# Second attention of a four-stage block: score passes of two heads as 64-row tiles, keys stored without zero halves

## The reference

```python
q = (x @ wq).reshape(B, T, H, D)              # H = 16 heads, D = 8, T = 256
lat = x @ w_down                              # 64 wide
k = (lat @ wk_up).reshape(B, T, H, D)
v = (lat @ wv_up).reshape(B, T, H, D)
q, k = _apply_rope(q, cos, sin), _apply_rope(k, cos, sin)
scores = jnp.einsum('bqhd,bkhd->bhqk', q, k) * scale
allowed = pages[None, :] <= pages[:, None]    # pages of 32 tokens
scores = jnp.where(allowed[None, None], scores, jnp.finfo(scores.dtype).min)
attn = jax.nn.softmax(scores, axis=-1)
out = jnp.einsum('bhqk,bkhd->bqhd', attn, v).reshape(B, T, E)
return out @ wo
```

## Time and profile before

| | us |
|---|---|
| median of 3 runs (lowest, highest) | 507.35 (506.74, 508.24) |
| the profiled execution | 500.75 |
| its span, first to last instruction | 498.9 |
| PE / VectorE (DVE) / ScalarE (ACT) / GpSimd (POOL) busy | 427.2 / 317.1 / 240.6 / 217.4 |
| mean granted clock of TensorE | 0.92 of full speed |

### The profile page before, as it was taken

One profiled execution on the slowest core, in us unless ns is written; L12 is line 12 of the kernel. 1 busy time (PEld: TensorE's weight loads), 2 busy tenths in 40 slices (PEclk: granted clock), 3 DMA queues, 4 the chain that ended last, 5 costly groups with the idle time before them and its releaser, 6 DMA issues.

```text
span 498.9 us, 15441 instructions
## 1 busy us (share of the span) xinstructions
PE 427.2 (86%) x5122; PEld 342.5 (69%) x5123; DVE 317.1 (64%) x1181; ACT 240.6 (48%) x575; POOL 217.4 (44%) x313
## 2 busy tenths in 40 slices
PE   8989899998668999976769989999899887899990
PEld 8767687886557899853546666666667666689980
DVE  4756588887554555279466567577777756555543
ACT  2676656765304555111325756657566440155540
POOL 5433345554633444324742625526531444334440
PEclk9989999997758999987678999999999997699996
DMA  8899900000001122120000000000000000112216
GB/s 263 273 210 347 292 13 11 6 11 12 23 16 44 55 63 63 55 57 1 2 1 1 1 3 2 0 0 0 1 1 3 18 28 22 32 51 64 63 47 179
DMA packets 43443, 29.12 MB, mean 58 GB/s; under 512 B 7200, under 2 KB 39456, under 8 KB 43264
## 3 DMA queue, kind: packets, MB, share of 16 engines
q1 hardware_dynamic: 37200, 21.35, 15.2%
q0 software_dynamic: 2496, 5.13, 2.8%
q10 hardware_dynamic: 3696, 1.97, 1.4%
HBM read 13.29 MB, written 15.16 MB: 57 GB/s over the span
## 4 chain that ended last, share of the span: by engine, by line
PE 60%; DVE 14%; issue 8%; ACT 7%; DMA 7%; DVEq 2%; POOL 2%; SPq 0%; ACTq 0%; POOLq 0%
PE S L1433 6%; PE S L1341 6%; PE bank L1300 6%; PE bank L1443 5%; PE bank L1317 3%; PE S L1520 3%; ACT E L1008 3%; PE S L1521 3%; PE bank L1473 3%; DMA slots<-yo,token 3%; PE bank L1533 2%; PE bank L1496 2%; PE bank L1327 2%; PE S L1273 2%; PE bank L1246 2%
## 5 line engine op out<-in xcount | busy, mean ns | idle before, releaser
L913 ACT ACTIVATE E<-S,nmax 128x256 f32<-128x256 f32 x128 | 59.0, 477 | 40.7 <-DVE nmax L541 38.0
L1148 POOL DMA_INDIRECT slots<-yo,token x46 | 44.1, 958 | 68.1 <-DVE yo L697 66.8
L1008 ACT ACTIVATE E<-S 128x1536 f32<-128x1536 f32 x32 | 46.4, 1451 | 25.3 <-PE S L1524 25.3
L1105 POOL TENSOR_TENSOR vs<-Va,rden 128x512 f32<-128x512 f32 x32 | 33.3, 1040 | 54.6 <-DVE rden L576 53.1
L1433 PE MATMUL S<-xgT,W1s 128*128 128x128 f32 x368 | 51.3, 282 | 1.4 <-DVE xgT L683 1.3
L757 DVE TENSOR_REDUCE nm<-bank 128x2 f32<-128x512 f32 x64 | 41.1, 683 | 15.9 <-PE bank L1496 15.9
L1443 PE MATMUL bank<-W,hT 128*128 x368 | 48.8, 276 | 0.2
L970 ACT ACTIVATE hT<-S,b 128x128 f32<-128x128 f32 x92 | 28.8, 363 | 40.5 <-PE S L1433 40.4
L1433 PEld LDWEIGHTS S<-xgT,W1s 128*128 128x128 f32 x368 | 44.5, 191 | 4.7 <-issue 2.2
L1443 PEld LDWEIGHTS bank<-W,hT 128*128 128x128 f32 x368 | 44.8, 192 | 0.5 <-issue 0.5
L541 DVE TENSOR_REDUCE nmax<-S 128x4 f32<-128x1024 f32 x32 | 39.0, 1218 | 8.6 <-PE S L1341 8.2
(11 more groups left out here) (182 smaller groups left out, 989.7 us busy)
## 6 DMA issues: line engine op xcount, KB each, us to landing
rows<-zeros SPq DMA_DIRECT2D x1, 8768.0 KB, 31.6
xg<-rows SPq DMA_DIRECT2D x46, 64.5 KB
W<-in_L_ffn_W SPq DMA_DIRECT2D x1, 2048.0 KB, 11.1
x<-in_L_attn_a_x SPq DMA_DIRECT2D x4, 256.0 KB, 5.3
yg<-in_select SPq DMA_DIRECT2D x1, 1024.0 KB, 9.2
yg<-slots SPq DMA_DIRECT2D x8, 128.0 KB, 3.7
yg<-slots ACTq DMA_DIRECT2D x8, 128.0 KB, 4.1
slots<-yo,token POOLq DMA_INDIRECT x46
```

The costliest lines, as they stand in the source:

```text
L913: last = act.activation(E[:, hp, h, c, :], S[hp % 2][:, h, c * T:(c + 1) * T], ACT.Exp, bias=nmax[:, hp, k:k + 1], accum_out=den[:, hp, k: ...
L1008: act.activation(Eb[:, q % 2, :, :], S4[:, 0:3, :], ACT.Exp, scale=SCALE_B).then_inc(bs["exp"], 1)
L1148: pool.indirect_dma_start(out=y_dram, out_offset=bass.IndirectOffsetOnAxis(token[:, turn_at, :], 0), in_=yo[:, turn_at % 2, :], in_offset=None
```

## The change

- `kT` loses its zero halves: one slot per pair, `kT[:, p, n, t]`. The memset of `keys` and the wait for it go. The first four pairs are copied over all 128 partitions by VectorE alone, the other four by ScalarE alone.
- Both score passes use 64-row tiles: rows 0 to 63 for head 0 of a pair, 64 to 127 for head 1.
- In the maximum pass the heads h=0 of two pairs share `pb[2]` and the heads h=1 share `pb[3]`; the four matmuls of 256 columns alternate between the halves. The third bank `S4[:, 3]` now holds four heads of the same h = q % 2 from the four pairs of a half batch, as four matmuls of 128 columns. The layout of `nm` follows, and the split of the maxima writes its parts to rows that match.
- The transposed block is issued in two halves. In the first, bank 0 is filled by h=0 and bank 2's h=1 parts beside it; in the second, bank 1 by h=1 and bank 2's h=0 parts. Bank 2 changes from one half of the rows to the other in between, and PE waits there for its own semaphore `low`.
- `sel` has 8 instead of 16 slots, so its DMA has half the bytes and its cast two pieces.

```diff
-            def b_kT(b, p, i):
+            def b_kT(b, p):
+                i = 0
                 dve.wait_ge(bs["tk"], b * 2 + i + 1)
-                src = pb[0][0:64, :].bitcast(BF16).rearrange("p (n t) -> p n t", n=4)
-                dve.tensor_copy(kT[0:64, p, 4 * i:4 * i + 4, 0, :], src).then_inc(bs["kT"], 1)
+                src = pb[0][:, :].bitcast(BF16).rearrange("p (n t) -> p n t", n=4)
+                dve.tensor_copy(kT[:, p, 4 * i:4 * i + 4, :], src).then_inc(bs["kT"], 1)
...
-            pool.wait_ge(a_scores, 4 * B)
-            pool.memset(keys[:, :], 0.0).then_inc(bs["zero"], 1)
...
                 before = (b * 4 + q) * 3 - 2
+                rows = [slice(64 * h, 64 * h + 64) for h in range(2)]
                 for d in range(2):
-                    n = 2 * q + d
-                    waits(pe, bs["max"], before + d)
-                    pe.matmul(pb[2 + d][:, :], qT[:, p, n, P:T], kT[:, p, n, :, :], start=True, stop=True
-                              ).then_inc(bs["s"], 1)
+                    for h in range(2):
+                        if d == 0:
+                            waits(pe, bs["max"], before + h)
+                        last = pe.matmul(pb[2 + h][:, d * T:(d + 1) * T], qT[rows[h], p, 2 * q + d, P:T],
+                                         kT[rows[h], p, 2 * q + d, :], start=True, stop=True)
+                        if d == 1:
+                            last.then_inc(bs["s"], 1)
                 waits(pe, bs["max"], before + 2)
-                for d in range(2):
-                    n = 2 * q + d
-                    last = pe.matmul(S4[:, 3, d * T:(d + 1) * T], qT[:, p, n, 0:P], kT[:, p, n, :, 0:P],
+                h = q % 2
+                for k in range(4):
+                    n = 4 * (q // 2) + k
+                    last = pe.matmul(S4[:, 3, k * P:(k + 1) * P], qT[rows[h], p, n, 0:P], kT[rows[h], p, n, 0:P],
                                      start=True, stop=True)
                 last.then_inc(bs["s"], 1)
...
+                def early(d, h, add):
+                    n, dst = 2 * q + d, S4[:, h, d * T:(d + 1) * T]
+                    if add:
+                        return pe.matmul(dst, sel[rows[h], n, :], mT[rows[h], :, :], start=False, stop=True)
+                    return pe.matmul(dst, kT[rows[h], p, n, 0:P], qT[rows[h], p, n, :], start=True, stop=False)
+
+                def late(d, h, add):
+                    n, dst = 2 * q + d, S4[:, 2, (2 * d + h) * P:(2 * d + h + 1) * P]
+                    if add:
+                        return pe.matmul(dst, sel[rows[h], n, :], mT[rows[h], 1, :], start=False, stop=True)
+                    return pe.matmul(dst, kT[rows[h], p, n, P:T], qT[rows[h], p, n, P:T], start=True, stop=False)
+
                 for d in range(2):
-                    for h in range(2):
-                        n, hh = 2 * q + d, 4 * q + 2 * d + h
-                        dst = S4[:, d, h * T:(h + 1) * T]
-                        pe.matmul(dst, kT[:, p, n, h, 0:P], qT[:, p, n, :], start=True, stop=False)
-                        pe.matmul(dst, sel[:, hh, :], mT[:, :, :], start=False, stop=True)
-                        dst = S4[:, 2, (2 * d + h) * P:(2 * d + h + 1) * P]
-                        pe.matmul(dst, kT[:, p, n, h, P:T], qT[:, p, n, P:T], start=True, stop=False)
-                        last = pe.matmul(dst, sel[:, hh, :], mT[:, 1, :], start=False, stop=True)
+                    early(d, 0, False)
+                    late(d, 1, False)
+                    last = late(d, 1, True)
+                    early(d, 0, True)
+                last.then_inc(bs["low"], 1)
+                for d in range(2):
+                    early(d, 1, False)
+                    if d == 0:
+                        pe.wait_ge(bs["low"], b * 4 + q + 1)
+                    late(d, 0, False)
+                    early(d, 1, True)
+                    last = late(d, 0, True)
                 last.then_inc(bs["st"], 1)
```

More of the change, by code:

```diff
@@ L158, in build @@
         yg = sb("yg", [P, NT, W])
-        sel = sb("sel", [P, HB, P], BF16)
+        sel = sb("sel", [P, HB // 2, P], BF16)
         identb = sb("identb", [P, P], BF16)
@@ L186, in build @@
             "p (a n t) -> p a n t", a=2, t=T)
-        kT = keys[:, :].bitcast(BF16).rearrange("p (a n h t) -> p a n h t", a=2, h=2, t=T)
+        kT = keys[:, :].bitcast(BF16)[:, 0:2 * 8 * T].rearrange("p (a n t) -> p a n t", a=2, t=T)
         Eb = E[:, :, :, :, :].rearrange("p s h c q -> p (s h c q)")[:, 0:2 * 3 * 512].rearrange(
@@ L228, in build @@
         bs = {k: sem(f"b_{k}") for k in
-              ("const", "chain0", "zero", "xb", "p1", "latT", "turnq", "p2", "turnk", "v", "vb", "chain", "split", "rep", "tq", "qT", "tk",
+              ("const", "chain0", "low", "xb", "p1", "latT", "turnq", "p2", "turnk", "v", "vb", "chain", "split", "rep", "tq", "qT", "tk",
                "kT", "kTa", "s", "max", "mchain", "ms", "mt", "mT", "st", "exp", "pv", "ot", "on", "rsum", "att",
@@ L245, in build @@
         block = ctx.enter_context(nc.Block())
-        copies = [(sel[:, 4 * k:4 * k + 4, :], yg[:, 4 * k:4 * k + 4, 0:D]) for k in range(4)]
+        copies = [(sel[:, 4 * k:4 * k + 4, :], yg[:, 4 * k:4 * k + 4, 0:D]) for k in range(2)]
         for t, name in ((qs, "qmask"), (ks, "kmask")):
@@ L794, in b_round @@
                     b_router(b, 0, (7,), router_second)
-                if n: b_kT(b + 1, 1 - p, 0)
+                if n: b_kT(b + 1, 1 - p)
                 if isinstance(b, int) and b == 5:
@@ L1026, in b_round @@
                 if c: b_outT(b, p, 0)
-                if n: b_kT(b + 1, 1 - p, 1)
+                if n: b_kT(b + 1, 1 - p)
                 if c: b_exp(b, 2)
@@ L1180, in b_maxima @@
                 waits(pool, bs["mt"], b)
-                parts = ms[:, :, 0:3 * HB].rearrange("p u (h k) -> p u h k", k=3)
+                parts = ms[:, :, :].rearrange("p u (h r) -> p u h r", h=2)[:, :, :, 0:3 * HB // 2].rearrange(
+                    "p u h (n k) -> p u h n k", k=3)
+                whole, less = [t[:, :, :].rearrange("p u (n h) -> p u h n", h=2) for t in (nm, nmr)]
                 chain.link(pool.tensor_tensor(
-                    parts[:, :, :, 0], nm[:, :, :], zeros[:, 0:2 * HB].rearrange("p (u h) -> p u h", u=2), ALU.add))
-                chain.inc(pool.tensor_tensor(nmr[:, :, :], nm[:, :, :], parts[:, :, :, 0], ALU.subtract))
-                chain.link(pool.tensor_tensor(parts[:, :, :, 1], nm[:, :, :], parts[:, :, :, 0], ALU.subtract))
-                chain.link(pool.tensor_tensor(parts[:, :, :, 2], nmr[:, :, :], parts[:, :, :, 1], ALU.subtract))
+                    parts[:, :, :, :, 0], whole, zeros[:, 0:2 * HB].rearrange("p (u h n) -> p u h n", u=2, h=2), ALU.add))
+                chain.inc(pool.tensor_tensor(less, whole, parts[:, :, :, :, 0], ALU.subtract))
+                chain.link(pool.tensor_tensor(parts[:, :, :, :, 1], whole, parts[:, :, :, :, 0], ALU.subtract))
+                chain.link(pool.tensor_tensor(parts[:, :, :, :, 2], less, parts[:, :, :, :, 1], ALU.subtract))
                 pool.sem_inc(bs["ms"], 1)
@@ L1533, in b_values @@
                     pe.matmul(pb[1][32 * h:32 * h + 32, 0:T], Vb[:, p, 0, 4 * q + h, :],
-                              Eb[:, q % 2, h // 2, (h % 2) * T:(h % 2 + 1) * T], start=True, stop=False)
+                              Eb[:, q % 2, h % 2, (h // 2) * T:(h // 2 + 1) * T], start=True, stop=False)
                 for h in range(4):
@@ L1707, in _select @@
 def _select():
-    s = np.zeros((P, HB, P), np.float32)
-    for h in range(HB):
-        s[3 * h:3 * h + 3, h, :] = 1.0
-    return s.reshape(P, HB * P)
+    s = np.zeros((P, HB // 2, P), np.float32)
+    for n in range(HB // 2):
+        for h in range(2):
+            s[64 * h + 3 * n:64 * h + 3 * n + 3, n, :] = 1.0
+    return s.reshape(P, HB // 2 * P)
 CST, NCST = {}, 0
```

28 lines of the change are left out of this document (14 added, 14 removed).

## The result

Before: 505.35 us median (502.58 to 510.84, 20 runs). After: 502.05 us (495.70 to 506.59, 20 runs). The ratio is 0.9905, 95% interval 0.9878 to 0.9932: 4.8 us off 505.35, faster, inside the range and a little under half of the 10.6 us forecast. All ratios of this study leave out the executions that took over 1.5% more than the fastest of the same kernel, here 7 of 20 after and 2 of 20 before; with all of them in, the two medians are 3.3 us apart. The profiled execution of the kernel after took 502.12 us with a span of 500.1, where that of before took 500.75 with 498.9. By these two profiles alone the change gained nothing, so the question is in which stretches they differ, and why.

What follows compares the result with a forecast made beforehand. TensorE, busy 86% of the span, was taken as the bound. Rounds 1 to 4 gave 5.6 us, the other terms brought 10.6; 500.75 became 490.15, and 6.6 added for the runs' median gave 496.8, range 489.5 to 504.0.

Steps and rivals of the forecast that it cites:

- rival B: Second attention: VectorE's maxima and rotation swallow half the gain; a round gains 0.65 us, time 502; chance 0.20.
- C: Score matmuls: bf16 tiles of two halves do not overlap; slower by 7 us, time 514; chance 0.07.
- D: Score matmuls: weight loads wait for their own half's running matmul; 27 us slower, time 534; chance 0.03.
- The block, 0.97 forecast: Transposed score block of a quarter: paired halves with a wait on `low` take 0.97 us instead of 1.33, -0.36.
- the release of `low`: Inside the block: PE waits until the first half's last matmul ends at 0.59, then starts 0.06 later, at 0.65.
- The steady round, 17.65 forecast: Second attention, one round between exponentials of quarter 0: 19.06 us becomes 17.65, -1.4 per round.
- The stall behind VectorE's maxima: Second part of pass 1 waits for pass 0's maxima in the same bank: a new stall of 0.28 us.
- A change of shape: Switching PE's tile shape costs 0.11 us; net 8 more in a round, 0.9 us of PE.
- round 6 an estimated -1.0: Second attention, round 6, where the router fills VectorE: an estimated gain of 1.0 us.
- batch 7 -0.3: Last round, without a pass for a next batch but with its changes of shape: gain of 0.3 us.
- rival E: PE's clock falls to 1.2 GHz for a quarter of each round, adding 10 us: time 507; chance 0.04.
- The 0.7 for the first round and the first attention: 0.4 us from the first round, and an estimated 0.3 from first attention's fewer `sel` casts and bytes.

Runs made afterwards that it cites:

- later_wait: Kernel after, with the score block's wait for `low` moved behind one more matmul: 499.02 us, ratio 0.9871.
- split_copies: Kernel after, with each group of keys copied half by VectorE and half by ScalarE, as before the change: 494.80 us, ratio 0.9859.
- pass_only: Kernel before, with only the maximum pass changed to 64-row tiles: 499.64 us, ratio 0.9981.
- block_only: Kernel before, with only the transposed block paired, `low`, and new layouts of `sel` and `ms`; keys keep zero halves: 497.80 us, ratio 0.9872.
- serial: Kernel after, with each block's matmuls ordered all of one row half, then all of the other: 499.63 us, ratio 0.9939.
- fill: Kernel after, with extra matmuls nobody reads put only in front of TensorE's long waits in rounds 5 to 7: 494.79 us, ratio 0.9853.
- later_fill: later_wait with the extra matmuls of fill in rounds 6 and 7 alone: 491.58 us, ratio 0.9827.
- again_before: Kernel before, unchanged, measured and profiled again: 504.96 us, ratio 0.996.
- serial67: Kernel after, with the matmul order of serial in rounds 6 and 7 alone: 492.74 us, ratio 0.9807.
- after_third: Kernel after, unchanged, measured a third time, beside later_fill on one chip: 498.88 us, ratio 0.9962.
- again_after: Kernel after, unchanged, measured and profiled again: 501.08 us, ratio 0.9859.
- Warm: Kernel after, with two extra matmuls nobody reads at the end of round 6 and five in round 7, in front of blocks: 501.15 us, ratio 0.9891.

## Why the prediction was half right

The number fell into the range, but not by the sum. The gain of the steady rounds came as forecast, a loss behind them that the sum did not have took half of it back, and 502.05 is the number of rival B (502), whose mechanism the rounds rule out. That it lies inside 489.5 to 504.0 is in part luck.

**What bounds the kernel, and whether the tiles overlap: right.** PE stayed the full engine (73.25 of 80 us for the 73.19 of the earlier trace rows). bf16 tiles of two halves run together, shown by the equal starts; rivals C and D are out. Against D stands the load of L1535 at 301.16: it starts 0.01 us after the L1536 of its own half (301.15, lasting 0.23), so it did not wait for it. A 64x128 bf16 load of L1530 took 97 ns on the mean, where I took 98 from the earlier trace rows.

**The block, 0.97 forecast, 0.92 measured: the step that read the release of `low`.** I let PE wait for the first half's last matmul and release at 0.65. In the code the signal sits on `late(1, 1, True)`, one matmul earlier (301.33, its record ends at 0.40), and PE went on at 0.57 (301.72), 0.17 behind it. For that step I had 0.06, read from another releaser: two errors of opposite sign. And the follower doesn't wait for the block's end but starts beside it on the other half, at 0.81: that I had missed.

**The steady round, 17.65 forecast, 17.45 measured.** Against the points I gave, counted from block 1: the second part of pass 1 at 1.42 (forecast 1.46); L1624 at 7.70 (7.81); L1468 at 8.55 (8.65); exponential 3 at 11.49 (11.65). From there to the next exponential 0 it was 4.74 and is 4.55, -0.19 for the -0.26 of block 0; and from exponential 0 to block 1, where pass 0 saves what its changes of shape cost, it is 1.51 in both. The stall behind VectorE's maxima is real: 302.57 is 0.61 behind the first L1502 at 301.96, where L1510 followed after 0.23 in pass 0, so 0.38 for my 0.28. A change of shape cost 0.10 (L1510 at 300.27 to L1476 at 300.58, less 0.21 of columns) for my 0.11. The Trainium skill (TensorEngine Tiling (Array Packing), Key Properties) says that a change of tiling mode drains TensorE; the trace agrees that there is a cost, and it is the 0.10, not a matmul's whole tail. Rival B, VectorE swallowing half, is out: its four rounds would have gained 2.6 us, they gained 6.4. So the terms of the steady rounds, 5.6 of my 10.6 us, were slightly too small.

**Rounds 6 and 7 and what follows: the steps that failed.** I gave round 6 an estimated -1.0 and batch 7 -0.3 by scaling from the steady rounds, and looked for rival E, the clock, between 280 and 360 us, where it stayed at 1.00. It fell behind that; measured are +0.1 and +3.2. In all three profiles of the kernel after, and in later_wait and split_copies, 7q0 to 7q3 takes 15.1 to 16.5 us with the clock low; where the clock held, it is 12.0 to 12.7 (the kernel before, pass_only, block_only, serial, fill, later_fill). again_before and serial67, with a clock that fell late in the stretch, lie between with 14.7 and 14.1. Most of the loss is in the last of the three steps, from 7q2 to 7q3; in the kernel after:

```profile
395.72 1.45 ACT L1012 ACTIVATE E<-S 128x1536 f32<-128x1536 f32 x1 [2.31 <-PE S L1535]
...
397.15 1.08 PE L1559 MATMUL bank<-E,Vb 128*32 128x256 f32 x8
...
404.15 1.45 ACT L1012 ACTIVATE E<-S 128x1536 f32<-128x1536 f32 x1 [1.26 <-PE S L1535]
```

This step takes 8.43 us at a granted 0.50 in the kernel after, 8.35 at 0.50 in later_wait, 8.16 at 0.51 in after_third, 7.90 at 0.57 in again_after, 7.63 at 0.55 in split_copies, 7.29 at 0.77 in again_before and 6.89 at 0.72 in serial67, and 5.2 to 5.5 at 1.00 in the six where the clock held; the two steps before it take 7.47 us in the kernel after and 7.29 in the kernel before. Warm is the exception: 7.16 us at 1.00 in this step, with the wait of L1628 and an extra matmul in it. Fill and later_fill turn the long stretch into the short one by work put into PE's waits. So the low clock costs some 3 us in batch 7 and 1 in round 6. That is rival E, to which I had given 0.04, at another place and at less than half of its price.

The largest part of what is missing is the +5.2 us behind 7q3, and it is not explained. 7q3 to the end takes 94.5 to 96.5 us in the three profiles of the kernel after and 90.7 to 93.4 in the six where the clock held; but again_before, the unchanged kernel, has 94.5, and split_copies, with the low clock in round 7, has 92.1. How much of this is the change I can't say.

Over whole runs the same shows: the mean granted clock is 0.927 in 76 runs of the kernel before (0.914 to 0.942) and 0.900 in the 38 of the kernel after (0.880 to 0.925). Within these 38, each taken against the mean of its own measurement, a run with 0.01 less took 1.9 us more (correlation -0.78). By that, 0.027 of clock goes with 5 us, about what is missing. A run that is long for another reason would show the same sign, so this is support and no proof; and later_fill, 7.3 us faster than the kernel after beside it, has a mean of 0.908 for 0.899, which by the same slope is 1.6 us of the 7.3.

**Why the clock falls there** is only partly open to view. PE's waits of half a microsecond and more from 5q0 to 7q0, in the kernel before: 0.59, 0.58, 1.09, 0.58 and 0.81, together 3.65 in 37.4 us. In the kernel after: 0.82, 0.78, 0.59, 1.27, 0.78 and 0.58, together 4.82 in 36.3 us. A faster block turned into longer waits there, since the router's rounds hang on other engines; that was rival E's own argument. It is not enough by itself: block_only has paired blocks too, waits 4.35 us in 35.7 with a longest wait of 1.25, and keeps 1.00 from 344 to 404. The longest of each kernel, before and after:

```profile
378.79 0.59 PE L1496 MATMUL bank<-keys,QT 128*128 128x512 bf16 x2 [1.09 <-issue]
```

```profile
371.73 0.39 PE L1502 MATMUL bank<-keys,QT 64*128 64x256 bf16 x4 [1.27 <-issue]
```

That filling them holds the clock is shown, in two profiles. Which of them is the one that matters, and why serial lost it in round 6 and serial67 at the end of round 7, is not settled.

**The base.** I measured the gain against a profile 6.6 us below the median shown of 507.35, and the median over 20 runs is 505.35. The forecast 496.8 stands on that too high base; against 505.35 the same 10.6 would have read 494.8, further from the result: an error of the base hid 2 us of the error of the sum. The gain itself is known to some us only: 0.9905, 0.9859 and 0.9962 in three measurements, which is 1.9 to 7.1 us, where the same kernel twice gave 0.996. Faster in all three, in the last within its interval of no change.

**The other parts.** Round 0 gained 1.8 for 2.0 (granted 0.66 from 256 to 264 us for the 0.50 of the earlier trace rows), round 5 1.3 for 1.0. The 0.7 for the first round and the first attention and the 0 for the memset can't be seen in the scatter of 10 us ahead of 0q0.

## What to carry to other kernels

When work is taken from TensorE in one stretch, list its waits in the neighbouring stretches as they will be afterwards, and look there for the granted clock, not only where the change is made: here the forecast was good to 0.2 us in a round of 17.5 and lost half its sum two rounds later. Where a wait of TensorE can't be removed, a few matmuls that nobody reads, put inside it and not in front of real work, held the clock and took 3.3 us off batch 7 and 1.3 off round 6, nearly as much as three steady rounds had gained; in round 5, where the clock had not fallen, they cost 1.1. Compare marks inside the profile (the same instruction of each round), since four steady rounds repeated to 0.02 us (69.81, 69.81, 69.79) where whole runs scatter by 2%.

## What the runs showed of the hardware

- Matmuls of the two row halves start out of program order. The L1536 at 301.27 stands behind an L1530 in the code that started at 301.38: each half runs ahead on its own. The Trainium skill (TensorE: Matmul & The Clock Gate, Part 3) says that matmuls are monotone in program order in start and end. For starts the trace differs; here nothing came of it: the signal sits on the block's last matmul in the code, an L1535, and the exponential that waits for it began at 302.27, when the record of the L1529 that started last (301.96 and 0.27) had ended.
- A switch between code lines is no boundary for it: L1502 of the next pass ran beside the last matmuls of the block (301.86 and 301.88 in serial), so the "serial" order kept more than half of the overlap: 1.00 us for 1.28 us of columns, where pairs take 0.81.
- A weight load did not wait for the running matmul of its own row half (301.16 beside 301.15).
- A change of tile shape between 64-row and full-array matmuls cost 0.10 us (300.27 to 300.58, less 0.21 of columns).
- At a granted 0.50 the eight records of L1559 took 1.08 us (at 397.15) for 0.64 at 1.00, and the step from 7q2 to 7q3 8.43 us for 5.38 in the kernel before.
